# Rows 3d to 3d+2 for a head's three terms in the stacks, and another spread of top-k's end

## The reference

```python
x = hidden_states                         # (8, 512, 256)
mod = (silu(c) @ wmod).reshape(8, 6, 1, -1)
sa, ca, ga, sb, cb, gb = (mod[:, i] for i in range(6))
ga, gb = sign(ga) * max(|ga|, 0.25), sign(gb) * max(|gb|, 0.25)
h = layernorm(x) * (1 + ca) + sa
# attention, 16 heads of 16
Q = (h @ Wq.T).reshape(b, t, 16, 16)
latent_k, latent_v = h @ Wk_down.T, h @ Wv_down.T          # 64 wide
q_lat = einsum('bthd,hdl->bthl', Q, q_to_latent)
logits = einsum('bthl,bsl->bhts', q_lat, latent_k) / 8     # causal
ctx = einsum('bhts,bsl->bhtl', softmax(logits), latent_v)
x = x + ga * (einsum('bhtl,hld->bthd', ctx, v_up).reshape(b, t, 256) @ Wout.T)
h = layernorm(x) * (1 + cb) + sb
# experts
scores = sigmoid(h @ gate_w.T)                             # (4096, 16)
topk_score, topk_ids = top_k(scores.T, 512)                # per expert
xin = h[topk_ids]
eo = silu(xin @ gw.T + gb_e) * (xin @ up_w.T + up_b)       # 1024 wide
eo = eo @ down_w.T + down_b
out = zeros.at[topk_ids].add(eo * topk_score)
shared = (silu(h @ sh_gate.T) * (h @ sh_up.T)) @ sh_down.T # 512 wide
x = x + gb * (out + shared)
```

## Time and profile before

| | |
|---|---|
| median of 3 runs | 1180.12 us (1177.16 to 1180.93) |
| the profiled execution | 1180.38 us |
| its span, first to last instruction | 1178.6 us |
| mean granted clock of TensorE | 0.966 |
| PE busy | 1120.8 us, 95% |
| DVE busy | 860.6 us, 73% |
| POOL, ACT busy | 633.5 us, 595.7 us |

### The profile page before, as it was taken

The page is one execution under the profiler, slowest core; times in us unless marked ns, Lnnn a source line. Parts: engine busy times, 40 slices in busy tenths (PEclk is TensorE's granted clock), DMA queues, the critical chain, the costliest instruction groups (busy, mean ns, idle before and its releaser), DMA issues.

```text
span 1178.6 us, 21664 instructions
## 1 busy us (share of the span) xinstructions
PE 1120.8 (95%) x7464; PEld 870.6 (74%) x7464; DVE 860.6 (73%) x2213; ACT 595.7 (51%) x1083; POOL 633.5 (54%) x669
## 2 busy tenths in 40 slices
PE   8889999999999898998889999999999999999997
PEld 5445656556556467887778888888888888888886
DVE  5687688888888579877957776767777667767562
ACT  2357667877876563221334455344455444454441
POOL 4124476676665543232435666665656565656644
PEclk8789799999999899999999999999999999999999
DMA  6647578878979444865345455655445655455631
GB/s 194 89 69 122 85 130 180 168 150 166 168 144 169 134 167 165 261 168 185 117 137 139 118 152 135 159 131 131 125 150 132 166 125 133 122 157 132 149 73 18
DMA packets 100333, 165.44 MB, mean 140 GB/s; under 512 B 18424, under 2 KB 65016, under 8 KB 98176
## 3 DMA queue, kind: packets, MB, share of 16 engines
q1 hardware_dynamic: 83360, 137.04, 46.2%
q0 software_dynamic: 14336, 25.70, 11.3%
q10 hardware_dynamic: 2528, 1.32, 0.8%
HBM read 103.71 MB, written 34.11 MB: 117 GB/s over the span
## 4 chain that ended last, share of the span: by engine, by line
PE 60%; DVE 11%; issue 8%; POOL 7%; DMA 6%; ACT 6%; ACTq 1%; SPq 0%; DVEq 0%; POOLq 0%
PE MB L552 14%; PE LB L552 14%; PE LB L866 8%; PE MB L866 7%; PE UB L682 4%; PE LB L644 3%; PE UB L552 3%; DMA QS<-NMl 3%; POOL out_y L1971 2%; PE XB L552 2%; DVE junk L1321 2%; PE MB L621 1%; ACT P L1016 1%; DMA XT<-hD 1%; ACT P L1018 1%
## 5 line engine op out<-in xcount | busy, mean ns | idle before, releaser
L1929 POOL TENSOR_TENSOR HTl<-HF,HTh 128x512 fp32r<-128x512 f32 x156 | 217.9, 1402 | 211.9 <-ACT HTh L1079 211.4
L1321 DVE CUSTOM_DVE_ANT_0 junk<-MB,MK 128x256 bf16<-128x256 f32 (+3 forms) x512 | 218.9, 483 | 50.9 <-PE MB L621 50.2
L1833 POOL TENSOR_SCALAR_AFFINE_SELECT P<-P 128x256 f32<-128x256 f32 x256 | 101.2, 419 | 163.7 <-ACT P L1018 163.5
L1971 POOL DMA_INDIRECT out_y<-EO,IDX x64 | 108.8, 1700 | 76.1 <-DVE EO L1789 66.0
L1090 ACT ACTIVATE SIL<-LB,gbT 128x512 f32<-128x512 f32 x64 | 44.0, 687 | 197.0 <-PE LB L552 191.8
L1016 ACT ACTIVATE P<-LB 128x768 f32<-128x768 f32 x128 | 104.0, 813 | 77.6 <-PE LB L644 76.0
L621 PE MATMUL MB<-KS,QS 48*128 48x256 f32 (+3 forms) x512 | 131.6, 366 | 9.3 <-DVE NM L1321 4.9
L644 PE MATMUL LB<-QS,KS 50*128 50x256 f32 (+3 forms) x512 | 125.4, 360 | 10.8 <-DMA QS<-NMl 6.0
L1079 ACT ACTIVATE HTh<-HF 128x512 fp32r<-128x512 f32 x156 | 98.0, 629 | 63.0 <-DVE HF L1690 62.8
L644 PEld LDWEIGHTS LB<-QS,KS 50*128 50x128 f32 x512 | 79.3, 191 | 60.2 <-issue 34.6
L621 PEld LDWEIGHTS MB<-KS,QS 48*128 48x128 f32 x512 | 81.2, 195 | 23.8 <-DVE NM L1321 12.3
(11 more groups left out here) (312 smaller groups left out, 3038.7 us busy)
## 6 DMA issues: line engine op xcount, KB each, us to landing
WR<-in_gw SPq DMA_DIRECT2D x16, 1024.0 KB
WR<-in_uw SPq DMA_DIRECT2D x16, 1024.0 KB
WR<-in_dw SPq DMA_DIRECT2D x16, 1024.0 KB
QS<-ST SPq DMA_DIRECT2D x96, 128.0 KB, 4.7
KS<-ST SPq DMA_DIRECT2D x90, 128.0 KB, 6.0
hD<-h SPq DMA_DIRECT2D x8, 1024.0 KB, 7.1
XT<-hD SPq DMA_DIRECT2D x7, 1024.0 KB, 8.3
X<-in_x SPq DMA_DIRECT2D x8, 512.0 KB, 6.5
```

The costliest lines, as they stand in the source:

```text
L1321: m = e.tensor_tensor_reduce(junk[:, o:o + w], MB[:, o:o + w], MK[:, 512 - w:512], 1.0, -3e38, ALU.add, ALU.max, NM[:, k // 4, 4 * (k % 4) ...
L1833: m = e.affine_select(out=dd, in_=dd, compare_op=ALU.is_ge, fill=0.0, base=0, pattern=[[0, 2], [1, 128]], channel_multiplier=-1)
L1929: e.tensor_tensor(HTl[:, slot, :], hf_of(n)[:], HTh[:, slot, :].bitcast(F32), ALU.subtract).then_inc(g_ht, 1)
L1971: e.indirect_dma_start(out=out2, out_offset=bass.IndirectOffsetOnAxis(ap=IDX[x_ % 3][:, q:q + 1], axis=0), in_=EO[:, q, :], in_offset=None ...
```

## The change

Two things change. First, the stacks: term r of column d of a head goes to row 3d + r instead of 16r + d, in QS and KS alike, so a transfer writes 16 partitions at stride 3. Number, size and order of the transfers stay, and so do rows 48 and 49.

Second, the end of top-k and what runs beside it:

- TensorE's matmul for the tie step is taken one step after VectorE's T_TIE, and T_POS, T_VAL and so on move back by a step; `values` for experts 1 to 15 is split into two steps; W_INDEX goes from 40 to 41.
- The cuts of expert 0's gate weights move from w = 39 to 42 to w = 18, 20, 22, 24; those of its up weights are at w = 42 to 45, with a wait for all of `values`, whose tiles they overwrite.
- Expert 0's down weights are loaded at w = 34 instead of 43; a block's XT is loaded one step earlier.
- The last block's residual and gate row get buffers of their own (XL7, GB7) and are loaded at w = 16.
- Expert 1's one-hots: two at w = 43 and 45, two in expert 0's first glus; expert 1's index one glu later.

```diff
@@ -32,7 +32,9 @@
 T_SEL = T_BIT + 31
-T_TIE, T_POS, T_VAL, T_HOT, T_VAL1, T_VAL2, T_END = (T_SEL + i for i in (1, 2, 3, 4, 6, 8, 9))
+T_TIE, T_POS, T_VAL, T_HOT, T_VAL1, T_VAL2, T_END = (T_SEL + i for i in (1, 3, 4, 5, 7, 8, 10))
+N_TIE, N_POS, N_VAL, N_ALL = (T_SEL + i for i in (2, 3, 4, 7))
@@ -55,8 +57,8 @@
 W_LOAD = 13
-W_PIECES = 39
-W_INDEX = 40
+W_CUTS = (18, 20, 22, 24, 42, 43, 44, 45)
+W_INDEX = 41
@@ -168,6 +170,9 @@
+    XL7 = at("XL7", 33664, [128, 4, D])
+    GB7 = at("GB7", 37760, [128, D])
     VR = at("VR", 69504, [128, 8])
@@ -215,7 +220,7 @@
     c_gbt, c_xl, c_out, c_sco, c_pos, c_scat = (sem(n) for n in ("c_gbt", "c_xl", "c_out", "c_sco", "c_pos", "c_scat"))
-    c_sd = sem("c_sd")
+    c_sd, c_l7 = sem("c_sd"), sem("c_l7")
@@ -329,7 +335,7 @@
                 for r, part in enumerate((0, 1, 0) if kind == 0 else (0, 0, 1)):
-                    e.dma_start(dst[base + 16 * r:base + 16 * r + 16, hs, :].bitcast(F32),
+                    e.dma_start(dst[base + r:base + 48:3, hs, :].bitcast(F32),
                                 src[64 * half:64 * half + 64, part, :].bitcast(F32)).then_inc(c_stack[2 * (u % 2) + half], 16)
@@ -470,7 +476,7 @@
             e.dma_start(outv[b], EO[:]).then_inc(c_out, 16)
-            if b + 1 < NB:
+            if b + 2 < NB:
                 load_xl(b + 1)
@@ -501,8 +507,14 @@
                 store_split(NB - 1)
-            if kind == "glu" and i == 1 and 3 <= b < NB - 1:
+            if kind == "glu" and i == 0 and 3 <= b < NB - 1:
                 load_h(b + 1)
+            if w == 16:
+                e.wait_ge(c_xd, 16 * NB)
+                e.wait_ge(g_sd, 2)
+                e.dma_start(GB7[:], modD[NB - 1, 5:6, :].broadcast_to([128, D])).then_inc(c_l7, 16)
+                e.dma_start(XL7[:], xD[NB - 1]).then_inc(c_l7, 16)
             if w == 15:
@@ -521,7 +533,7 @@
                 e.dma_start(WR[1][:].rearrange("p (k n) -> p k n", k=2), kn(uw[0])).then_inc(c_wr[1], 16)
-            if w == W_PIECES + 4:
+            if w == 34:
                 load_piece(piece_d(0), dw[0])
@@ -813,11 +825,12 @@
                 e.matmul(XB[:, 2:3], Lm, PT[:, 511:512], start=True, stop=True).then_inc(p_top, 1)
-            elif t == T_TIE:
-                e.wait_ge(d_top, t + 1)
+            elif t == T_TIE + 1:
+                e.wait_ge(d_top, N_TIE)
                 e.matmul(XB[:, 3:4], Lm, PT[:, 511:512], start=True, stop=True).then_inc(p_top, 1)
             elif t == T_POS:
-                e.wait_ge(d_top, t + 1)
+                e.wait_ge(d_top, N_POS)
                 for k in range(4):
@@ -873,7 +886,7 @@
-            e.wait_ge(d_top, T_VAL + 3 if x_ else T_VAL + 1)
+            e.wait_ge(d_top, N_ALL if x_ else N_VAL)
             for k in range(32):
@@ -937,7 +950,7 @@
                 glu(n_eglu(x_, m_) - 1, m_, WG[x_ % 2], WU[x_ % 2], XT[x_ % 2], no_tick)
-                if nxt and m_ == 1:
+                if nxt and m_ == (1 if x_ else 2):
                     index(x_ + 1)
@@ -1102,7 +1115,7 @@
             for r, part in enumerate((0, 0, 1)):
-                e.dma_start(KS[16 * r:16 * r + 16, 4 * half:4 * half + 4, :].bitcast(F32),
+                e.dma_start(KS[r:48:3, 4 * half:4 * half + 4, :].bitcast(F32),
                             ST[1][64 * half:64 * half + 64, part, :].bitcast(F32)).then_inc(c_stack[half], 16)
@@ -1235,8 +1248,8 @@
                 flush()
-            if W_PIECES <= w < W_PIECES + 8:
-                j = w - W_PIECES
+            if w in W_CUTS:
+                j = W_CUTS.index(w)
                 cut(piece_g(0) + j // 4, j % 4)
@@ -1620,13 +1633,13 @@
                 if t == T_HOT:
-                    e.wait_ge(d_top, T_VAL + 1)
+                    e.wait_ge(d_top, N_VAL)
                 onehot(0, 2 * (t - T_HOT))
                 rows(slice(1, NE), d_top)
-            elif t == T_VAL2:
-                values(slice(1, NE))
+            elif t in (T_VAL2, T_VAL2 + 1):
+                values(slice(1, NE), range(2 * (t - T_VAL2), 2 * (t - T_VAL2) + 2))
@@ -1642,8 +1655,8 @@
-        def values(es):
-            for q in range(4):
+        def values(es, qs=range(4)):
+            for q in qs:
                 e.tensor_scalar(of(V4[:, q, 0, :], es), of(GT[:], es), float(q), VR[:, 0:1], ALU.is_equal, ALU.mult)
@@ -1696,13 +1709,18 @@
             e.wait_ge(p_down, n)
-            e.wait_ge(c_gbt, 16 * (b + 1))
-            e.tensor_tensor(tb[q % 2][:], (LB, MB)[q % 2][:, 1024:1280], GBt[:], ALU.mult).then_inc(d_tb, 1)
+            last = b == NB - 1
+            if last:
+                e.wait_ge(c_l7, 32)
+            else:
+                e.wait_ge(c_gbt, 16 * (b + 1))
+            e.tensor_tensor(tb[q % 2][:], (LB, MB)[q % 2][:, 1024:1280], (GB7 if last else GBt)[:], ALU.mult).then_inc(d_tb, 1)
             e.wait_ge(d_tb, n)
-            e.wait_ge(c_xl, 16 * (b + 1))
+            if not last:
+                e.wait_ge(c_xl, 16 * (b + 1))
             if b:
                 e.wait_ge(c_out, 16 * b)
-            e.tensor_tensor(EO[:, q, :], tb[q % 2][:], XL[:, q, :], ALU.add).then_inc(d_eo, 1)
+            e.tensor_tensor(EO[:, q, :], tb[q % 2][:], (XL7 if last else XL)[:, q, :], ALU.add).then_inc(d_eo, 1)
@@ -1756,23 +1774,29 @@
                     shared_down(b, q)
-            if W_PIECES <= w < W_PIECES + 8:
-                j = w - W_PIECES
+            if w in W_CUTS:
+                j = W_CUTS.index(w)
+                if j == 4:
+                    e.wait_ge(d_top, N_ALL)
                 cut(e, piece_g(0) + j // 4, j % 4)
-            if w in (42, 43, 44, 45):
-                onehot(1, w - 42)
+            if w in (43, 45):
+                onehot(1, (w - 43) // 2)
         for x_ in range(NE):
                 glu(n_eglu(x_, m_) - 1, m_, ubT[:, x_, m_:m_ + 1])
+                if x_ == 0 and m_ < 2:
+                    onehot(1, 2 + m_)
                 if m_ < 4:
                     cut(e, piece_d(x_), m_)
-                if nxt and m_ == 1:
+                if nxt and m_ == (1 if x_ else 2):
                     index(x_ + 1)
                     cut(e, piece_g(x_ + 1), m_ - 4)
-                if x_ + 2 < NE and 2 <= m_ < 5:
-                    onehot(x_ + 2, m_ - 2)
+                if x_ + 2 < NE and (2 if x_ else 3) <= m_ < (5 if x_ else 6):
+                    onehot(x_ + 2, m_ - (2 if x_ else 3))
                 if nxt and m_ >= 6:
@@ -1961,7 +1985,7 @@
                     glu(n_eglu(x_, m_ - 1) - 1, m_ - 1, m_ - 1, n_edown(x_, 0) - 1)
-                if m_ == 1 and x_ + 1 < NE:
+                if m_ == (1 if x_ else 2) and x_ + 1 < NE:
                     index(x_ + 1)
```

## The result

| | median us | profiled execution, span |
|---|---|---|
| before | 1180.47 (1177.16 to 1180.93) | 1178.6 |
| changed | 1166.12 (1162.91 to 1169.99) | 1165.8 |

The ratio is 0.9885, with a 95% interval of 0.9845 to 0.9925: 13.6 us less, between 9 and 18. Two further comparisons of the same two kernels, each on another chip, gave 0.9836 (0.9795 to 0.9877) and 0.9862 (0.9827 to 0.9896). The mean of the three is 0.986, or 16.4 us. The forecast was 19.2 us and 0.984. The changed kernel is faster, by somewhat less than forecast.

A forecast was written before the change was run, and what follows sets the result against it. TensorE was taken as the bound, with VectorE the bound between 556 and 592 us. From 1180.4 us, 10.9 for top-k's end and 8.3 for the stack rows gave 1161.2 us, range 1152 to 1171.

The forecast's parts named there:

- (c): Middle of top-k's end: waits for one-hots and tb go, 1.9 us for HF stays; gain 3.0 us; gathers apart, -1.0.
- (e): Fill of the pipeline: TensorE's waits for the two halves of the stacks shrink; gain 3.1 us, between 0 and 5.
- (a): Start of block 6: its input, loaded one step earlier, no longer comes late; gain 0.8 us.
- (b): Tie count in top-k's end: asked for later, wait falls to 0.6 us and half clock goes; gain 3.4 us.
- (d): Last block's residual and gate: early loads remove a 3.5 us standstill and the half clock after it; gain 5.2 us.
- The cuts near 500 us: Four weight cuts moved to 495 to 515 us, mostly into VectorE's idle time; cost 0.5 us, between 0 and 3.8.
- The two one-hots moved into expert 0: In expert 0, where VectorE has a quarter of its time free: they cost nothing.
- (f): Row maxima in attention: most waits for their 8 KB transfers vanish as stack bursts land sooner; gain 5.2 us.
- Rival C: Attention, 128 to 145 us: shorter standstills keep the clock up, 6 us more, 1155; with the fill 1153; chance 0.12.
- A: Stack bursts: no faster, because DMA engines hold them; only the top-k gains are left, 1169.5 us; chance 0.14.
- B: End of top-k: the spread only moves the standstills, its gain falls to 5.5 us, time 1166.6; chance 0.11.
- D: Stack transfers: strided rows hinder each other, bursts land 1.4 us later, time 1199 us; chance 0.05.

The follow-up runs named there:

- e1: The kernel before with only the stack rows changed to stride 3: 1171.03 us, ratio 0.9923.
- e6: The changed kernel with TensorE asking for the tie count in the tick of before, not three later: 1170.11 us, ratio 0.9920.
- e4: The changed kernel with block 7's residual and gate row loaded late again, behind the store of block 6's output: 1167.85 us, ratio 0.9917.
- e2: The changed kernel with the old stack rows (16r+d), so only the spread of top-k's end: 1172.46 us, ratio 0.9926.
- e11: The changed kernel run again without edits, against the kernel before on another chip: 1162.90 us, ratio 0.9862.
- e0: The changed kernel run again without edits, against the kernel before on another chip: 1161.79 us, ratio 0.9836.
- e5: The changed kernel with four weight cuts back at w = 38 to 41 and the dw load at 42: 1168.07 us, ratio 0.9901.
- e9: The changed kernel with stack rows at stride 4, in stacks of 64 rows: 1159.24 us, ratio 0.9822.
- e7: The changed kernel with HF ahead of top-k's ticks from w = 40 and HTl ahead of expert 0's gathers: 1165.18 us, ratio 0.9886.
- e3: The changed kernel with groups of SBUF-to-SBUF copies behind its end, to compare row layouts alone: 1356.21 us, including the copies.

## Why the prediction was right, and where it wasn't

The time was right: 1161.2 us forecast, 1166.12, 1161.79 and 1162.90 measured in the three comparisons. That it was so near owes something to luck. The two steps that failed, (c) and (e), were short by 6.5 us of the 19.2, which leaves 12.7. The three profiled executions of the changed kernel are 12.8, 13.7 and 16.4 us shorter than that of before, and the ratios give 16.4 in the mean. No term accounts for the 2 to 4 us between. Point by point:

(a) XT: 0.8 forecast. Block 6's first glu starts with no wait, and the way to it from block 5's first glu is 18.6 us instead of 19.6. But e1, which issues this load as before, has no wait there either and the same 18.6 us. So whether the earlier issue won the 0.8 isn't shown.

(b) The tie count, 3.4: e6 gives 3.4. Right, with 0.33 us of wait left where 0.6 was forecast and no half clock behind it.

(d) The preload, 5.2: e4 gives 5.2, by other parts, as said above. Right in its sum. "VectorE's tb is done before TensorE needs it" was wrong, though: two waits for tb, 2.1 us, stand in the changed kernel.

(c) The middle, with the gathers: forecast +3.0 and -1.0. 58.4 less 51.2 is 7.2, less (b) and (d), 8.6, leaves a loss of 1.4. This is the first step that failed, by 3.4 us. The walk through VectorE's queue had HF of (7, 0) done at s + 28.3; it was done at 566.90, s + 30.0. Two terms of it were too small. The four one-hots took 5.7 us instead of 4.8 (553.13 to 558.8): the first, beside GpSimd's HTl at 552.80, took 2.31 us, the others 1.21. And the rows of the other experts took 3.4 us instead of 2.4. Then the walk stopped at (7, 2). Behind it VectorE has four cuts, two one-hots and a wait of 2.6 us for GpSimd, and that is where the 2.1 us for tb come from. I had counted GpSimd's gathers as late, but not what was queued behind them. The half clock forecast behind the HF wait (0.9) didn't come in this execution; in e2, behind the same 2.8 us, it did (0.83 from 570 to 580 us). It cost nothing that shows: the way from s is 51.0 us in e2 and 51.6 here, since the waits for tb and XG behind it are shorter there (1.7 us instead of 3.5).

The cuts near 500 us: 0.5 forecast, waits for jk 0.9 instead of 0.7, and some 0.6 us in the distances between blocks. Right.

The two one-hots moved into expert 0: nothing, I said. In the changed kernel and e11 that is so; e0, e2, e5 and e9 have a wait of 1.0 to 1.8 us for expert 1's gathers there. A small cost that I had not seen.

(e) The fill: 3.1 forecast, nothing measured. This step failed too. The changed kernel's first matmul for the exponential is at 53.71 us instead of 54.54, but e2, with the old rows, has it at 53.36, and the ten executions at stride 3 have it between 52.64 and 55.01, 54.0 in the mean, which is also the mean of the two at adjacent rows. The waits for KS fell from 2.01 to 0.41 and from 1.58 to nothing, but behind the first stands ScalarE's xh, ready at 33.9 us in both traces. e9 fits: with no wait for KS left, that matmul is at 53.56. I had not asked what is late next.

(f) The maxima: 5.2 forecast. The mean end of attention is 423.8 at stride 3 and 429.7 at adjacent rows (before and e2), 5.8 us, with only two executions on one side. Most of the scatter is the clock. If the time lost at half clock is taken off (half of each such stretch up to attention's end, from the clock's records in the traces), attention ends at 398.0 and 399.9 us at adjacent rows, at 393.2 to 394.6 in nine executions at stride 3 and 391.3 in the tenth (e6), and at 391.8 and 391.7 at stride 4. So the rows are worth 5.1 us without the clock, none of it in the fill. Right, and the one burst of the earlier trace rows gave the sign and the size. A part that reaches the time by way of the clock is not shown: it cost 32.4 and 29.0 us at adjacent rows and 23.9 to 35.8, 30.0 in the mean, at stride 3. TensorE's longest standstills at the end of attention, before and in e7, and the clock behind the second (columns as above):

```profile
386.85 0.38 PE L644 MATMUL LB<-QS,KS 50*128 50x256 f32 x1 [2.17 <-DMA QS<-NMl]
```

```profile
392.38 0.38 PE L656 MATMUL LB<-QS,KS 50*128 50x256 f32 x1 [1.13 <-ACT P L1029]
```

```profile
388.00:408.00 20.00, 18.79 (x91) 10.37 (x83) 8.97 (x27) 10.19 (x19) 10.86 (x15) 0.66 0.27 85
```

Before, the clock was 0.74 in that stretch, in e7 0.66, and in e0 1.00, where no wait between 380 and 400 us is longer than 0.7 us. Rival C had looked for a gain of the clock at 128 to 145 us, where nothing changed (0.83 from 120 to 160 us in both).

The rivals: A falls by e1 and e3. Rival A had also a rule of the Trainium skill (DMA: Bandwidth & Descriptors, "Queues, rings and completion order"), that an engine changes between the queues after each packet. What the prediction drew from it, that (f) would shrink to a part, did not come. The maxima's transfers landed after a median of 3.8, 2.7 and 1.9 us as SyncE's bursts sped up at equal bytes. Whether they waited for one packet, which was slow itself, or for a part of the backlog no run here separates; so the rule itself is neither borne out nor refuted. B was right in its first part, the standstill of the middle moved on, and wrong in its second, since (b) was won whole. D, strided rows that hinder each other, has nothing for it: all landings are shorter.

## What to carry to other kernels

Where small copies to few partitions hold up an engine, spread the rows of each copy evenly over the groups of four partitions: alone, stride 4 nearly doubled the rate of 16 rows (213 instead of 118 GB/s), stride 3 gave only a seventh (135), and the rows added to the matmul cost nothing that showed. When a wait is taken away, walk on through every queue until the next engine is late, not only to the next wait: here (c) and the fill fell short for that. Measure a step by the distance between two fixed operations of the trace; it agreed to 0.8 us between executions, where the ratios leave 3 us or more. And don't read the gain of a step from one pair of traces: the 0.8 us that the pair gives for (a) and for (e) did not stand up to the other traces.

## What the runs showed that I had not expected

The same code, stride 3 in attention, ended it anywhere between 418.5 and 428.2 us. Nearly all of that is the clock over the whole of attention, as the figures under (f) show. One place of it is 380 to 420 us: the clock is 1.00 in e4 and e0, 0.82 and 0.84 in e7, behind a single wait of 1.1 us. The prediction had read from one trace that no half clock stands behind waits of 0.8 to 1.2 us; here 13.7 us of it do, and behind the 2.8 us for HF in the changed kernel none. So a gain of 3 us can hide or be feigned in one profile.

VectorE's operations stretch beside GpSimd's: a cut of 0.68 us took 2.44 and an addition of 0.42 took 1.34 (changed kernel, VectorE, with a gather of GpSimd from 575.11 us and its HTl at 576.07 and 580.41):

```profile
575.49 2.44 DVE L1823 TENSOR_TENSOR WU0l<-WR,WU0h 128x512 fp32r<-128x512 f32 x1
...
580.63 1.34 DVE L1723 TENSOR_TENSOR EO<-tb,XL 128x256 f32<-128x256 f32 x1
```

The Trainium skill (SBUF - State Buffer, "Who interferes with whom") says that the two share a pair of ports, which one instruction holds to its end. The second row agrees: HTl ended at 581.70, and the addition 0.27 us later. The first doesn't settle it: the cut began 0.58 us ahead of HTl and ended 0.56 us behind its end at 577.37.
